# Keys and values of a cross-attention: one unsplit float32 product in place of three split ones

## The reference, cut to what matters

```python
    def _L0_xattn_ref(q, kv, Wq, Wk, Wv, Wo, bo):   # q: layer-normed x, kv: ctx_512 (16, 128, 128)
        ...                                        # NUM_HEADS = 16, HEAD_DIM = 64, INNER = 1024
        scale = HEAD_DIM ** (-0.5)
        qh = (q @ Wq).reshape(B, N, NUM_HEADS, HEAD_DIM).transpose(0, 2, 1, 3)
        kh = (kv @ Wk).reshape(B, M, NUM_HEADS, HEAD_DIM).transpose(0, 2, 1, 3)
        vh = (kv @ Wv).reshape(B, M, NUM_HEADS, HEAD_DIM).transpose(0, 2, 1, 3)
        scores = jnp.einsum('bhnd,bhmd->bhnm', qh, kh) * scale
        attn = jax.nn.softmax(scores, axis=-1)
        out = jnp.einsum('bhnm,bhmd->bhnd', attn, vh)
        out = out.transpose(0, 2, 1, 3).reshape(B, N, INNER)
        return out @ Wo + bo
```

## Time and profile before

| | us |
|---|---|
| median of 3 runs (lowest, highest) | 647.48 (646.87, 647.78) |
| the profiled execution | 647.54 |
| its span, first to last instruction | 645.7 |
| TensorE busy in it | 635.5 (98%) |
| VectorE | 502.9 (78%) |
| ScalarE | 413.8 (64%) |
| GpSimd | 350.4 (54%) |
| stage A, B, C roughly | to 279, 279 to 540, from 523 |

### The profile page before, as it was taken

One profiled execution on the slowest core, in us unless ns is written; L12 is line 12 of the kernel. 1 busy time (PEld: TensorE's weight loads), 2 busy tenths in 40 slices (PEclk: granted clock), 3 DMA queues, 4 the chain that ended last, 5 costly groups with the idle time before them and its releaser, 6 DMA issues.

```text
span 645.7 us, 16043 instructions
## 1 busy us (share of the span) xinstructions
PE 635.5 (98%) x5339; PEld 549.3 (85%) x5339; DVE 502.9 (78%) x976; ACT 413.8 (64%) x1454; POOL 350.4 (54%) x745
## 2 busy tenths in 40 slices
PE   9899999999999999999999999999999999999998
PEld 4688888888888888887888888888888888888987
DVE  4888789988998889976777777766667758888765
ACT  2688888888888888876555557465655453444432
POOL 4997476666676566865587766555356532010100
DMA  7955000000000000032100000000000000000010
GB/s 218 376 238 197 0 3 2 2 1 0 0 0 0 0 1 0 16 131 66 47 2 17 3 2 1 18 2 3 1 0 0 0 1 2 1 34 12 20 35 32
DMA packets 10437, 23.93 MB, mean 37 GB/s; under 512 B 1666, under 2 KB 6066, under 8 KB 9490
## 3 DMA queue, kind: packets, MB, share of 16 engines
q1 hardware_dynamic: 7794, 14.63, 6.6%
q0 software_dynamic: 1872, 7.87, 3.5%
q10 hardware_dynamic: 720, 0.79, 0.4%
HBM read 21.19 MB, written 2.10 MB: 36 GB/s over the span
## 4 chain that ended last, share of the span: by engine, by line
PE 92%; DVE 3%; ACT 3%; issue 1%; POOL 0%; DVEq 0%; ACTq 0%; POOLq 0%
PE bank L561 21%; PE bank L563 20%; PE bank L562 20%; PE bank L759 5%; PE bank L649 5%; PE bank L747 5%; PE bank L735 5%; PE bank L626 5%; PE bank L615 3%; PE bank L579 2%; PE bank L568 1%; PE bank L880 1%; ACT e_sb L1040 1%; DVE ri L1192 1%; DVE hid L1436 0%
## 5 line engine op out<-in xcount | busy, mean ns | idle before, releaser
L438 POOL TENSOR_SCALAR p_f<-e_sb,rsum 128x128 f32<-128x128 f32 x256 | 91.0, 373 | 85.2 <-DVE rsum L1381 84.8
L346 POOL TENSOR_SCALAR p_int<-e_sb,rsc 128x128 int16<-128x128 f32 x256 | 106.8, 434 | 6.7 <-issue 6.2
L1040 ACT ACTIVATE e_sb<-bank,neg_max 128x128 f32<-128x128 f32 x256 | 90.3, 385 | 4.0 <-DVE neg_max L1337 4.0
L953 ACT ACTIVATE sgn<-bank 128x512 bf16<-128x512 f32 x96 | 54.5, 606 | 34.5 <-PE bank L563 34.4
L968 ACT ACTIVATE e_sb<-si 128x128 f32<-128x128 int16 x256 | 76.5, 316 | 0.0
L1192 DVE SCALAR_TENSOR_TENSOR ri<-sgn,bank 128x512 int16<-128x512 bf16 x96 | 63.4, 685 | 14.2 <-ACT sgn L953 12.7
L1058 ACT ACTIVATE q_sb<-bank 128x512 f32<-128x512 f32 x32 | 19.2, 600 | 75.5 <-PE bank L563 75.5
L1040 ACT ACTIVATION_READ_ACCUMULATOR e_sb<-bank,neg_max 128x1 f32 x256 | 57.8, 226 | 0.0
L968 ACT ACTIVATION_READ_ACCUMULATOR e_sb<-si 128x1 f32 x256 | 53.1, 207 | 0.0
L561 PE MATMUL bank<-xnT_hi,wqk_lo 128*128 128x512 f32 x128 | 52.8, 413 | 0.0
L563 PE MATMUL bank<-xnT_hi,wqk_hi 128*128 128x512 f32 x128 | 50.2, 392 | 0.0
(11 more groups left out here) (154 smaller groups left out, 2118.4 us busy)
## 6 DMA issues: line engine op xcount, KB each, us to landing
wB_raw<-in_wB SPq DMA_DIRECT2D x1, 3072.0 KB, 13.7
wB_hi<-in_wB POOLq DMA_DIRECT2D x1, 3072.0 KB, 11.3
wqk_raw<-in_wqk SPq DMA_DIRECT2D x8, 256.0 KB, 7.6
wqk_hi<-in_wqk POOLq DMA_DIRECT2D x7, 256.0 KB, 8.2
x_sb<-in_x SPq DMA_DIRECT2D x3, 512.0 KB, 19.9
out<-x_sb SPq DMA_DIRECT2D x6, 256.0 KB, 2.3
wp_raw<-in_wp SPq DMA_DIRECT2D x1, 1024.0 KB, 14.9
wp_hi<-in_wp POOLq DMA_DIRECT2D x1, 1024.0 KB, 9.1
```

The source lines that it names most:

```text
L346: i = nc.gpsimd.tensor_scalar(p_int[:, half, t, :], e_sb[:, half, t, :], rsc[:, half, t:t + 1], -0.5, ALU.mult, ALU.add)
L438: i = nc.gpsimd.tensor_scalar(p_f[:, half, t, :], e_sb[:, half, t, :], rsum[:, half, t:t + 1], 0.0, ALU.mult, ALU.add)
L953: nc.scalar.activation(sgn[:, m % 2, :], proj_ps[m % 2][:, :], ACT.Sign).then_inc(a_sgn, 1)
L1040: last = nc.scalar.activation(e_sb[:, (s - 1) % 2, t, :], s_ps[hh][:, (t % 4) * P:(t % 4 + 1) * P], ACT.Exp, bias=neg_max[:, t:t + 1], sca ...
```

## The change

The keys and values of stage B are no longer made of split products:

- Keys: one float32 product of 512 columns for three split ones. Values: two float32 products of 256 columns for six split ones. Both read the loaded contexts and the raw Wk and Wv.
- `cT_raw`, `cT_hi` and `cT_lo` are gone, and with them the casts and subtractions of the contexts on ScalarE, VectorE and GpSimd and the semaphores `b_chi` and `b_clo`. One tile `cT_sb` holds the contexts of all four groups, each with its own load semaphore. SyncE issues the loads of groups 0 to 2 where the first one stood, and that of group 3 at the end of stage A.
- The chunks of `wB` are reordered (Wq, Wo, Wk, Wv). `wB_hi` and `wB_lo` have four chunks, `wB_raw` keeps six, the cast load brings four, and GpSimd makes four: those of group 3 of stage A fall away. TensorE waits for `wB_done` 4.
- Three tiles of stage C are placed elsewhere (over the raw Wk and Wv). TensorE's loop over groups 2 and 3 of stage B is written out, since the wait for a group's context names its semaphore; the loops of the other engines stay.

```diff
-    wB_hi = sb("wB_hi", [P, 6, E], F32R)
-    wB_lo, wB_at, _ = place("wB_lo", [P, 6, E], F32R)
+    wB_hi = sb("wB_hi", [P, 4, E], F32R)
+    wB_at = mem["at"]
...
-    wB_raw = sb("wB_raw", [P, 6, E], F32, at=wB_at)
+    wB_raw = sb("wB_raw", [P, 6, E], F32)
+    wB_lo = sb("wB_lo", [P, 4, E], F32R, at=wB_at)
...
-    cT_raw, _, nxt = place("cT_raw", [P, TOK], F32, at=nxt)
-    cT_hi, _, nxt = place("cT_hi", [P, TOK], F32R, at=nxt)
-    cT_lo, _, nxt = place("cT_lo", [P, TOK], F32R, at=nxt)
+    cT_sb, _, nxt = place("cT_sb", [P, G, TOK], F32, at=nxt)
...
-    wk_hi, wk_lo = wB_hi[:, 2, :], wB_lo[:, 2, :]
-    wvB_hi, wvB_lo = wB_hi[:, 3, :], wB_lo[:, 3, :]
+    wkB, wvB = wB_raw[:, 4, :], wB_raw[:, 5, :]
...
             sp.wait_ge(a_blk, BLOCKS * (G - 1) + 18)
-            sp.dma_start(cT_raw[:, :], ctxT[:, 0:TOK]).then_inc(ld_ctx, 16)
+            for g in range(G - 1):
+                sp.dma_start(cT_sb[:, g, :], ctxT[:, g * TOK:(g + 1) * TOK]).then_inc(ld_ctx[g], 16)
             sp.wait_ge(a_blk, BLOCKS * G)
+            sp.dma_start(cT_sb[:, G - 1, :], ctxT[:, (G - 1) * TOK:G * TOK]).then_inc(ld_ctx[G - 1], 16)
...
-                if last and s == 6:
-                    pool.wait_ge(ld_ctx, 16)
-                    nc.gpsimd.tensor_copy(cT_hi[:, :], cT_raw[:, :]).then_inc(b_chi, 1)
-                    pool.wait_ge(b_chi, 1)
-                    minus_high(cT_lo, cT_raw, cT_hi, TOK).then_inc(b_clo, 1)
-                if not first and s in (0, 2):
+                if not first and not last and s in (0, 2):
...
-                    nc.gpsimd.dma_start(wB_hi[:, :, :], wB).then_inc(lh_wB, 16)
+                    nc.gpsimd.dma_start(wB_hi[:, 0:4, :], wB[:, 0:4, :]).then_inc(lh_wB, 16)
...
                 elif what == "k":
                     wait(pe, b_q, NP * g + s + 1)
-                    last = split3(one_ps[:, :], [w[:, s * P:(s + 1) * P] for w in (wk_hi, wk_lo)],
-                                  [t[:, :] for t in (cT_hi, cT_lo)], True, True)
+                    last = pe.matmul(one_ps[:, :], wkB[:, s * P:(s + 1) * P], cT_sb[:, g, :], start=True, stop=True)
                 else:
                     wait(pe, b_pT0, NP * g + s - LAG + 1)
                     if s == 0:
-                        wait(pe, b_clo, g + 1)
+                        pe.wait_ge(ld_ctx[g], 16)
...
-                        last = split3(v_ps[:, i * QW:(i + 1) * QW], [t[:, b * P:(b + 1) * P] for t in (cT_hi, cT_lo)],
-                                      [w[:, col:col + QW] for w in (wvB_hi, wvB_lo)], i == 0, True,
-                                      skip_group_check=True)
+                        last = pe.matmul(v_ps[:, i * QW:(i + 1) * QW], cT_sb[:, g, b * P:(b + 1) * P], wvB[:, col:col + QW],
+                                         start=i == 0, stop=True, skip_group_check=True)
...
-            with pe.Fori(2, G) as g:
+            for g in range(2, G):
...
-                    if s == 0 and not first:
-                        wait(act, ld_ctx, 16 * (g + 1))
-                        wait(act, b_blk, BLOCKS * g)
-                        nc.scalar.copy(cT_hi[:, :], cT_raw[:, :]).then_inc(b_chi, 1)
...
-                if s == 0 and not first and not drain:
-                    wait(dve, b_chi, g + 1)
-                    V.tensor_tensor(cT_lo[:, :], cT_raw[:, :], cT_hi[:, :].bitcast(F32), ALU.subtract).then_inc(b_clo, 1)
```

More of the change, by code:

```diff
@@ L115, in build @@
     top_sb = sb("top_sb", [P, 2], F32)
+    idx_sb = sb("idx_sb", [1, 2], I32)
     cw_hi, _, nxt = place("cw_hi", [P, 4, F], F32R, at=region_a)
@@ L120, in build @@
     p_f, _, nxt = place("p_f", [P, 2, 8, NT], F32, at=nxt)
-    cT_raw, _, nxt = place("cT_raw", [P, TOK], F32, at=nxt)
-    cT_hi, _, nxt = place("cT_hi", [P, TOK], F32R, at=nxt)
-    cT_lo, _, nxt = place("cT_lo", [P, TOK], F32R, at=nxt)
-    idx_sb, _, nxt = place("idx_sb", [1, 2], I32, at=nxt)
+    cT_sb, _, nxt = place("cT_sb", [P, G, TOK], F32, at=nxt)
     assert nxt <= region_p
@@ L139, in build @@
     relu1, _, nxt = place("relu1", [P, TOK], F32, at=nxt)
-    hid, _, nxt = place("hid", [P, 2, TOK], F32, at=nxt)
     lowT, _, nxt = place("lowT", [96, TOK], F32R, at=nxt)
+    assert nxt <= region_b + 4 * 2 * E
+    hid, _, nxt = place("hid", [P, 2, TOK], F32, at=wB_at + 4 * 4 * E)
     oT2_hi, _, nxt = place("oT2_hi", [P, TOK], F32R, at=nxt)
     oT2_lo, _, nxt = place("oT2_lo", [P, TOK], F32R, at=nxt)
-    assert nxt <= region_b + 4 * 4 * E
+    assert nxt <= wB_at + 4 * 6 * E
     tile_hi, tile_lo = (oT2_hi, oT_hi), (oT2_lo, oT_lo)
@@ L172, in build @@
     ld_wp, ld_b, ld_bb, ld_top, out_done = (sem(n) for n in ("ld_wp", "ld_b", "ld_bb", "ld_top", "out_done"))
-    ld_wB, ld_ctx, ld_idx = sem("ld_wB"), sem("ld_ctx"), sem("ld_idx")
+    ld_wB, ld_idx = sem("ld_wB"), sem("ld_idx")
+    ld_ctx = [sem(f"ld_ctx{g}") for g in range(G)]
     ld_wi, ld_wd, ld_la, ld_la0, ld_lb = (sem(n) for n in ("ld_wi", "ld_wd", "ld_la", "ld_la0", "ld_lb"))
@@ L176, in build @@
     w0_hi, w0_lo, w_lo, wB_done, g_tick = sem("w0_hi"), sem("w0_lo"), sem("w_lo"), sem("wB_done"), sem("g_tick")
-    b_chi, b_clo, b_blk, b_q, b_k, b_v = (
-        sem(n) for n in ("b_chi", "b_clo", "b_blk", "b_q", "b_k", "b_v"))
+    b_blk, b_q, b_k, b_v = (sem(n) for n in ("b_blk", "b_q", "b_k", "b_v"))
     b_pT0 = sem("b_pT0")
@@ L226, in build @@
     wq_hi, wq_lo = ([w[:, i, :] for i in range(KD)] for w in (wB_hi, wB_lo))
-    wk_hi, wk_lo = wB_hi[:, 2, :], wB_lo[:, 2, :]
-    wvB_hi, wvB_lo = wB_hi[:, 3, :], wB_lo[:, 3, :]
-    wo_hi, wo_lo = (w[:, 4:6, :].rearrange("p a (t d) -> p (a t) d", d=D) for w in (wB_hi, wB_lo))
+    wkB, wvB = wB_raw[:, 4, :], wB_raw[:, 5, :]
+    wo_hi, wo_lo = (w[:, 2:4, :].rearrange("p a (t d) -> p (a t) d", d=D) for w in (wB_hi, wB_lo))
     def merge_chunk(c):
@@ new lines, in _ @@
+            sp.dma_start(wi_raw[:, :, :], wiT).then_inc(ld_wi, 16)
+            sp.dma_start(wd_raw[:, :, :], wdT).then_inc(ld_wd, 16)
+            sp.wait_ge(a_pj, NP * G)
+            sp.wait_ge(ld_idx, 16)
+            for k in range(2):
+                expert = sp.value_load(idx_sb[0:1, k:k + 1], min_val=0, max_val=lora_AT.shape[0] - 1)
+                sp.dma_start(la_raw[:, :, k * RANK:(k + 1) * RANK],
+                             lora_AT[bass.ds(expert, 1), :, :, :].rearrange("a p k r -> p (a k) r")).then_inc(ld_la, 16)
+                if k == 0:
+                    sp.wait_ge(g_la0, 1)
+                for j in range(3):
+                    at = 32 * j + k * RANK
+                    if k == 0:
+                        sp.dma_start(la0_raw[at:at + RANK, :],
+                                     lora_A[bass.ds(expert, 1), :, :].rearrange("a r d -> (a r) d")).then_inc(ld_la0, 16)
+                    sp.dma_start(lb_raw[at:at + RANK, :],
+                                 lora_BT[bass.ds(expert, 1), :, :].rearrange("a r f -> (a r) f")).then_inc(ld_lb, 16)
@@ L697, in _ @@
                     a_slot(g, s)
-            pe.wait_ge(wB_done, 6)
+            pe.wait_ge(wB_done, 4)
             def b_block(g, s, what):
@@ L1485 @@
         "wB": np.concatenate([given["L0_xattn_Wq"].reshape(KD, P, E).transpose(1, 0, 2),
-                              given["L0_xattn_Wk"][:, None, :], given["L0_xattn_Wv"][:, None, :],
-                              given["L0_xattn_Wo"].reshape(NP, P, D).transpose(1, 0, 2).reshape(P, 2, E)], axis=1),
+                              given["L0_xattn_Wo"].reshape(NP, P, D).transpose(1, 0, 2).reshape(P, 2, E),
+                              given["L0_xattn_Wk"][:, None, :], given["L0_xattn_Wv"][:, None, :]], axis=1),
         "bo": given["L0_xattn_bo"],
```

## The result

| | before | after |
|---|---|---|
| median, us | 647.52 | 655.68 |
| profiled execution | 647.54 | 655.54 |
| its span | 645.7 | 653.5 |
| ratio of the times | | 1.0156, 95% interval 1.0109 to 1.0202 |

The changed kernel is slower by 8.2 us (medians); 656.3 was forecast, 654.5 to 661.5 the range.

A forecast was written before the change was run, and what follows sets the result against it. The prediction took TensorE to bound the cross-attention's steady slots. From the profiled 647.54 us, +9.9 for float32 blocks, -0.6 for two ScalarE waits and -0.5 for a group boundary gave 656.3 us, range 654.5 to 661.5.

The forecast's parts named there:

- The bound: Cross-attention: in steady slots TensorE never waits, so each nanosecond added to its stream is added to the kernel.
- Four passes: Key and value blocks: a float32 product costs two records, each passing its columns twice, four times a single pass.
- the two rows it names: Bfloat16 warm-up products of 512 columns (0.216 us) and transposes of 128 (0.055 us), used to price one pass.
- The first rival: Key and value blocks: float32 products take half the passes, -17.6 us, total 630.5 us; chance 0.07.
- the smaller cost in between: Float32 runs: 0.055 us extra after each first record, +3.5 us, total 659.8 us; chance 0.14 shared with surplus.
- The second rival: Key and value blocks: float32 records carry the split products' surplus, +15.7 us, total 662.1 us; chance 0.14 shared with start-up cost.
- The halving for FP32_LOW_HIGH: Array output rate falls only by 2, which would change the sum's sign; 630.5 us, chance 0.07.
- The term of +9.9 us: Key and value blocks on TensorE: +0.31 us a slot over 32 slots of the cross-attention.
- The savings: Cross-attention: waits shortened elsewhere, -0.6 us at the scores and -0.5 us at one group boundary; other deleted work priced at nothing.
- Two waits for ScalarE: Slots 1 and 2 of group 0: scores' waits for exponentials each swallow 0.31 us of the longer blocks, -0.6 us.
- The boundary of groups 1 and 2: Values wait there for VectorE's late copy; deleting the context subtraction in front of it removes the wait, -0.5 us.
- gave nothing for the loop: TensorE, groups 2 and 3: looped and written-out slots take 7.38 and 7.37 us, so writing it out gains nothing.

The follow-up runs named there:

- the two blocks alone: Kernel before with only the values, or only the keys, made of unsplit float32 products (high parts only): 651.84 and 651.98 us, against 647.21.
- both: Kernel before with values and keys unsplit (high parts only), old loads, casts, subtractions and loop kept: 656.58 us against 647.21, ratio 1.0129.
- the loop alone: Kernel before with only TensorE's loop over groups 2 and 3 of the cross-attention written out: 647.35 us against 647.60, ratio 0.9996.
- new rest: Changed kernel with three float32r products for each float32 one, so TensorE's stream is that of before: 646.34 us against 647.21, ratio 0.9977.

## Why the prediction was right

**The bound.** TensorE without slack in the slots: the slots grew by 0.30 us for two blocks that grew by 0.145 and 0.166 us (means of slots 2 to 6 of group 2, start to start), and the two blocks alone add up (4.07+4.65 = 8.72 us against 8.93 for both).

**Four passes.** Forecast: records at 0.216 and 0.429 us, four and two a slot, slots of 7.69 us, 96 records fewer. Measured: 0.215 and 0.433 us, four and two, 7.67 to 7.69 us, 96. The prediction's 0.417 ns a column and 0.0025 us an instruction do not quite follow from the two rows it names (0.216 and 0.055 us give 0.419 ns and 0.0013 us), but the records come out the same to 0.001 us either way. The first rival (half the passes, 630.5 us) is out by these pitches. So is the smaller cost in between (a first record followed late, 659.8 us): the first two value records of a slot are 0.21 us apart and the two key records 0.43. The second rival (surplus, 662.1 us) was priced well for float32r: the kernel with four float32r passes came to 660.6 us, but float32 records have next to none of it. The page "FP8 and Floating Point Precision" of the Trainium skill, section "TensorE Precision Notes", is borne out with its four passes for true FP32: 0.433 us for 512 columns in each of two records, against 0.216 us for one bfloat16 pass. The halving for FP32_LOW_HIGH in the page "Perfetto Trace Analysis" of the Trainium skill, section "Engine Utilization", is not what a float32 product costs here.

**The size.** The term of +9.9 us was 0.4 too large. Over the slots of group 2 the mean went from 7.39 to 7.69 us, +0.297, x32 = +9.5. The two blocks together were right (+0.311 us); the split products of the projection, which follow, run at 0.119 instead of 0.120 us in the changed kernel, and that gives back 0.012 us a slot, 0.4 in all. I had not looked for an effect on neighbours.

**The savings.** Two waits for ScalarE: the gaps from attend to scores went from 0.90 and 0.96 to 0.58 and 0.63 us, -0.65 against -0.6. The boundary of groups 1 and 2: 7.18 us became 6.90 where the other slots grew by 0.3, which is -0.58: the wait of 0.5 us and 0.07 that the loop had cost there. 9.5-0.65-0.58 = 8.3 us, and the cross-attention grew by 8.25. The prediction compared two steady slots and gave nothing for the loop; at its two group boundaries it cost 0.07 and 0.05 us (the loop alone, above), which is below what the time can tell. The new rest is worth 0.74 us of the cross-attention in all: 0.58 at that boundary, 0.04 at the next. The prediction also took the waits of the earlier trace rows for all of TensorE's waits. The one in slot 3 of group 0 (0.3 us, behind VectorE's copy) and a smaller one in slot 4 (0.14 us) are not in that view; they are the same before and after, so the sum did not suffer.

**What stays open.** The last 0.1 us of the new rest may be GpSimd's and ScalarE's deleted work or scatter, and why the projection runs faster behind float32 products is not known; these runs do not tell.

## What to carry to other kernels

Count passes before choosing a format: on a TensorE-bound path one float32 product is four passes and a three-term float32r split is three somewhat dearer ones, so unsplitting lost 0.30 us a slot, however much it tidies away on engines that had slack. Before making the bound engine's work shorter, read how long before its use the next engine's result is ready; here that slack was 0.22 us in a steady slot, and of 0.95 us a slot saved on TensorE 0.4 came back in the mean (646.34 to 633.96 us over 32 slots) until one line of ScalarE's order was changed.

## What the runs showed of the hardware

- A float32 product leaves two records, full array or tiled. On the full array a record takes 0.215 us for 256 columns and 0.433 for 512, the latter twice the 0.216 us of a bfloat16 record of 512, so each record costs two passes. A float32 transpose of 128 columns leaves one record and takes 0.109 us.
- float32r products of 512 columns mostly run at 0.23 to 0.235 us, those of 256 at 0.12; bfloat16 in the place of the keys at 0.216. The surplus of 6 to 9% at 512 columns belongs to float32r, its weight loads included. I had carried it as a possible cost of float32, where it is 1% at most.
- After a float32 run, the next split product's first record begins 0.03 us after the last float32 one and its second 0.31 us later; summed, nothing is lost. A pitch taken from a single such record would mislead. So would one taken across a missing record, as in the bfloat16 keys: counting the weight loads shows it.
